# A last expert phase with eight slots cut in two halves of 64 rows, 19 slots in place of 22

## The reference

```python
logits = xf @ Wg
top_w, top_i = jax.lax.top_k(logits, TOP_K)              # TOP_K = 2, E = 8
top_w = jax.nn.softmax(top_w, axis=-1)
one_hot = jax.nn.one_hot(top_i, E, dtype=xf.dtype)
combine = jnp.einsum('nk,nke->ne', top_w, one_hot)
h = jnp.einsum('nc,ech->enh', xf, W1)                    # 256 -> 512
g = jnp.einsum('nc,ech->enh', xf, W2)
y = jnp.einsum('enh,ehc->enc', jax.nn.silu(h) * g, W3)   # 512 -> 256
out = jnp.einsum('enc,ne->nc', y, combine)
```

## Time and profile before

| | us |
|---|---|
| Runs shown (3) | 504.51, 506.26, 506.55; median 506.26 |
| Profiled execution, time | 505.15 |
| Its span | 503.4 |
| PE busy | 439.5 (87%) |
| DVE busy | 281.0 (56%) |
| ACT busy | 206.0 (41%) |
| POOL busy | 166.6 (33%) |

### The profile page before, as it was taken

One profiled execution on the slowest core, in us unless ns is written; L12 is line 12 of the kernel. 1 busy time (PEld: TensorE's weight loads), 2 busy tenths in 40 slices (PEclk: granted clock), 3 DMA queues, 4 the chain that ended last, 5 costly groups with the idle time before them and its releaser, 6 DMA issues.

```text
span 503.4 us, 9416 instructions
## 1 busy us (share of the span) xinstructions
PE 439.5 (87%) x3418; PEld 282.7 (56%) x3419; DVE 281.0 (56%) x853; ACT 206.0 (41%) x385; POOL 166.6 (33%) x140
## 2 busy tenths in 40 slices
PE   0889899798778856878899999999999999999991
PEld 0545456456455645646557666666666666566651
DVE  0498786686869999998975767346411111111110
ACT  1234653463587424246426632453333333333330
POOL 6051010010101044631434455443544442554322
PEclk9999999999967956898999999999999999999997
DMA  8999210046045100732005222341333225333211
GB/s 174 255 210 211 58 40 3 9 132 241 19 155 210 44 7 1 276 143 85 26 28 126 42 43 43 101 69 20 50 46 53 42 42 187 63 45 50 41 21 21
DMA packets 36103, 43.16 MB, mean 86 GB/s; under 512 B 5216, under 2 KB 30560, under 8 KB 35904
## 3 DMA queue, kind: packets, MB, share of 16 engines
q1 hardware_dynamic: 26384, 32.14, 22.9%
q0 software_dynamic: 7488, 10.23, 12.9%
q10 hardware_dynamic: 2192, 0.27, 0.5%
HBM read 30.96 MB, written 11.53 MB: 84 GB/s over the span
## 4 chain that ended last, share of the span: by engine, by line
PE 65%; DVE 17%; issue 5%; DMA 5%; ACT 4%; SPq 3%; POOLq 0%; DVEq 0%; ACTq 0%
PE psum L2257 26%; PE psum L2276 13%; PE psum L1874 9%; DMA M3s<-in_x_dram 4%; PE psum L2267 3%; PE psum L1888 3%; PE psum L1900 2%; PE psum L2247 2%; PE psum L1918 2%; DVE st_att L1028 1%; SPq L316 1%; DVE H L1271 1%; DVE qtok L1188 1%; DVE Eb L1068 1%; DMA out_dram<-O,dst_i 1%
## 5 line engine op out<-in xcount | busy, mean ns | idle before, releaser
L1771 DVE TENSOR_TENSOR QT<-QT,psum 128x512 f32<-128x512 f32 x39 | 26.8, 687 | 136.9 <-PE psum L2257 136.9
L2276 PE MATMUL psum<-M3s,KT 128*128 x312 | 74.1, 380 | 1.3 <-ACT KT L822 0.8
L2257 PE MATMUL psum<-M1s,KT 128*128 x156 | 74.0, 597 | 1.1 <-issue 0.8
L2257 PE MATMUL psum<-M2s,KT 128*128 x156 | 73.3, 592 | 0.0
L2276 PEld LDWEIGHTS psum<-M3s,KT 128*128 128x128 f32 x312 | 58.6, 190 | 22.1 <-issue 16.1
L833 ACT ACTIVATE O<-psum,gate_slot 128x256 f32<-128x256 f32 x39 | 18.5, 474 | 106.7 <-PE psum L2276 106.7
L1874 PE MATMUL psum<-M2s,M1s 128*128 128x512 f32 x128 | 58.7, 602 | 0.8 <-ACT H L688 0.7
L503 POOL DMA_INDIRECT KT<-mixture_rows_in,src_i x39 | 42.6, 1093 | 33.0 <-issue 19.7
L2257 PEld LDWEIGHTS psum<-M2s,KT 128*128 128x128 f32 x156 | 29.6, 190 | 37.3 <-issue 37.3
L530 POOL DMA_INDIRECT mixture_rows_out<-O,src_i x17 | 30.8, 1813 | 33.1 <-ACT O L833 13.3
L818 ACT ACTIVATE QT<-psum 128x512 f32<-128x512 f32 x39 | 23.3, 596 | 39.8 <-PE psum L2257 39.7
(11 more groups left out here) (407 smaller groups left out, 747.1 us busy)
## 6 DMA issues: line engine op xcount, KB each, us to landing
M3s<-in_x_dram SPq DMA_DIRECT2D x4, 1024.0 KB, 11.8
M3s<-in_L_ffn_W_dram SPq DMA_DIRECT2D x1, 4096.0 KB, 15.1
M2s<-in_L_ffn_W_dram SPq DMA_DIRECT2D x1, 4096.0 KB, 15.4
M1s<-in_L_ffn_W_dram SPq DMA_DIRECT2D x1, 4096.0 KB, 15.1
M3s<-in_x_dram SPq DMA_DIRECT2D x4, 992.0 KB, 15.7
M1s<-vtok SPq DMA_DIRECT2D x64, 34.0 KB, 1.9
mixture_rows_out<-H SPq DMA_DIRECT2D x4, 512.0 KB, 4.1
M1s<-in_L_tok_W_dram SPq DMA_DIRECT2D x2, 512.0 KB, 14.2
```

The costliest lines, as they stand in the source:

```text
L1771: v.tensor_tensor(sil[:, u, :], sil[:, u, :], bank[3], ALU.mult).then_inc(v_gated, 1)
L2257: last = mm(z, xrT[:, u, c, :], w[:, bass.ds(e, 1), c, :].rearrange("p a h -> p (a h)"), start=(c == 0), stop=(c == CH - 1))
L2276: last = mm(bank[6][:, 0:DM], actT[:, u, c, :], M3s[:, bass.ds(e, 1), c, :].rearrange("p a d -> p (a d)"), start=(c == 0), stop=(c == HC - 1))
```

## The change

The last phase gets 19 slots in place of 22, so there are 36 in all. Eight of them (`HALVED`: 17, 18, 20, 21, 23, 24, 26, 28) are cut: rows 0 to 63 have an expert that is looked up, rows 64 to 127 have a fixed one, expert n in the n-th such slot. Eleven are whole; four of these (19, 22, 25, 27) stand between the cut ones, seven (29 to 35) behind. `COLUMN` maps a slot's place in time to its column in the tables.

On PE each up and down product of a cut slot is issued as two matmuls, one for each half of 64 columns of the array (`experts`, and the loop over `rows`). A cut slot is delivered by two DMAs of 64 rows, `deliver` and `deliver_high`; the second waits until the first has landed, as every delivery does. `MIXED` is 29, so the copy comes after slot 28. Around it POOL takes other fetches first: no delivery stands in turn 30, and from turn 31 on delivery j-2 follows fetch j+3.

The block arithmetic is longer, the positions are moved twice (`move_left`), rows are respread (`spread_halves`) and `rows_hot` is done anew for all four groups of tiles. `places2` for the last tiles moves from behind the activations of step 12 to behind the up products of step 11; the one-hot tables move from step 13 to 14, the table matmul from step 14 to 15, the gates from 15 to 16. Slot 17's fetch, its transposes and its ACT copy come at the end of step 15, behind the down product.

```diff
-    SLOTS = (2 * NTOK + E * (P - 1)) // P
...
-    REST = SLOTS - FULL
-    WHOLE = REST - E
-    MIXED = FULL + E
+    HP = P // 2
+    WHOLE = 2 * NTOK // P - FULL - E // 2
+    REST = E + WHOLE
+    SLOTS = FULL + REST
+    ORDER = "TTWTTWTTWTWT"
+    MIXED = FULL + len(ORDER)
+    HALVED = [FULL + n for n, kind in enumerate(ORDER) if kind == "T"]
...
-            sp.wait_ge(d_deliver, 16 * MIXED)
+            sp.wait_ge(d_deliver, delivered(MIXED - 1))
...
+            def deliver_high(j):
+
+                pool.wait_ge(d_deliver, delivered(j) - 16)
+                gp.indirect_dma_start(acc, bass.IndirectOffsetOnAxis(ap=dst_high[:, COLUMN[j] - FULL:COLUMN[j] - FULL + 1], axis=0),
+                                      yrow[HP:P, j % 4, :], None, compute_op=ALU.add).then_inc(d_deliver, 16)
...
             for j in range(SLOTS):
-                if j + 3 < SLOTS:
+                split = j - 1 in HALVED
+                if split:
+                    deliver(j - 1)
+                if j + 2 == FULL:
+                    fetch(FULL)
+                if j + 3 < SLOTS and not (j + 3 == FULL):
                     fetch(j + 3)
...
-                if j > 0:
+                if split:
+                    deliver_high(j - 1)
+                elif 0 < j <= MIXED:
                     deliver(j - 1)
+                elif j > MIXED + 1:
+                    deliver(j - 2)
+            deliver(SLOTS - 2)
             deliver(SLOTS - 1)
...
-                if j + 2 < SLOTS:
+                if j + 2 < SLOTS and not (j + 2 == FULL):
                     slot_rows(j + 2, u)
...
                 slot_out(j)
+                if j + 2 == FULL:
+                    slot_rows(j + 2, u)
...
                 if j == 13:
-                    move_last(TILES)
-                    pair_slots(TILES)
-                    wrap_slots()
-                    slots_hot(2, TILES, REST, far_slot)
+                    positions(TILES, ALU.is_le, R_lim, W_at)
+                    move_left(TILES)
+                    pair_slots(TILES, halves=True)
+                if j == 14:
+                    slots_hot(2, TILES, REST, slot_in)
                     table_tiles(2, TILES, REST)
-                if j == 14:
-                    rows_of(FIRST, TS)
-                    rows_hot(3)
+                    rows_of(0, TILES)
+                    for i in range(STEPS - 1):
+                        rows_hot(i)
+                if j == 15:
+                    rows_hot(last)
                     rest_experts()
...
+            def experts(j):
+
+                n = COLUMN[j] if isinstance(j, int) else j
+                e = bass.ds(pe.value_load(exi[0:1, bass.ds(n, 1)], min_val=0, max_val=E - 1), 1)
+                if isinstance(j, int) and j in HALVED:
+                    return [(slice(0, HP), e), (slice(HP, P), slice(n - FULL, n - FULL + 1))]
+                return [(slice(0, P), e)]
...
                     for c in range(CH):
-                        last = mm(z, xrT[:, u, c, :], w[:, bass.ds(e, 1), c, :].rearrange("p a h -> p (a h)"),
-                                  start=(c == 0), stop=(c == CH - 1))
+                        for rows, e in parts:
+                            last = mm(z[rows, :], xrT[:, u, c, rows], w[:, e, c, :].rearrange("p a h -> p (a h)"),
+                                      start=(c == 0), stop=(c == CH - 1))
...
-                if j == 12:
-                    places2(2, FIRST, TILES, 1, bank[1])
...
+                if j == 11:
+                    places2(2, FIRST, TILES, 1, bank[1])
+                if j == 16:
                     gate_columns(2, TILES, REST, bank[7])
...
-                if isinstance(j, int) and j == 14:
+                if late_rows:
                     slot_tables(2, TILES, REST, bank[1])
...
                 slot_down(j, u)
+                if late_rows:
+                    slot_rows(j + 2, u, loads)
```

More of the change, by code:

```diff
@@ L298, in audio_tower_kernel, with delivered @@
         NORM2_ACT = 2
+        def delivered(j):
+            return 16 * (j + 1 + sum(h <= j for h in HALVED))
         def step_of(slot, lag):
@@ L367, in _ @@
             sp.wait_ge(d_copied, 16)
-            sp.wait_ge(d_deliver, 16 * SLOTS)
+            sp.wait_ge(d_deliver, delivered(SLOTS - 1))
         @block.gpsimd
@@ L831, in slot_out @@
                     act.wait_ge(v_gate_slot, 3)
-                wait(act, d_deliver, 16 * (j - 3))
-                a.activation(yrow[:, j % 4, :], bank[6][:, 0:DM], ACT.Copy, scale=gate_slot[:, j:j + 1]
+                wait(act, d_deliver, delivered(j - 4))
+                a.activation(yrow[:, j % 4, :], bank[6][:, 0:DM], ACT.Copy, scale=gate_slot[:, COLUMN[j]:COLUMN[j] + 1]
                              ).then_inc(a_slot_out, 1)
@@ L1466, in ranks, with whole @@
                 return ln(v.tensor_copy(ra[:, 7, lo:lo + n, :], z[:, 0:n * E].rearrange("p (t e) -> p t e", e=E)))
-            def whole(out, counts, half):
-                own(ln(v.tensor_scalar(out, counts, half, P * MAGIC, ALU.add, ALU.add)))
-                own(ln(v.tensor_scalar(out, out, P * MAGIC, 1.0 / P, ALU.subtract, ALU.mult)))
+            def whole(out, counts, half, rows=P):
+                own(ln(v.tensor_scalar(out, counts, half, rows * MAGIC, ALU.add, ALU.add)))
+                own(ln(v.tensor_scalar(out, out, rows * MAGIC, 1.0 / rows, ALU.subtract, ALU.mult)))
             def first_slots(counts, n, ts):
@@ L1582, in rest_blocks @@
[L1582 to L1585 removed]
+                whole(F, counts, -(P - 1) / 2)
+                own(ln(v.tensor_tensor(F_new, F, used, ALU.subtract)))
+                own(ln(v.tensor_tensor_scan(F_end, ones_e[:], F_new, 0.0, ALU.mult, ALU.add)))
+                own(ln(v.tensor_tensor(F_off, F_end, F_new, ALU.subtract)))
@@ new lines, in rest_blocks @@
+                ln(v.tensor_tensor(W_off, W_end, blocks, ALU.subtract))
+                own(ln(v.tensor_scalar(H_lim, W_lim, float(HP), None, ALU.add)))
+                ln(v.scalar_tensor_tensor(H_at, expert_no[:], float(P), H_lim, ALU.mult, ALU.subtract))
+                own(ln(v.tensor_tensor(over, counts, H_lim, ALU.subtract)))
+                ln(v.tensor_scalar(W_at, W_off, float(P), float(P * E - 1), ALU.mult, ALU.add))
+                own(ln(v.tensor_scalar(over, over, 0.0, None, ALU.max)))
@@ L1610, in pair_slots, with spread_halves @@
                 own()
+                if halves:
+                    spread_halves(n)
                 whole(slot_in[:, :, 0:n], rs[:, 5:7, 0:n], -(P - 1) / 2)
-            def wrap_slots():
-                ln(v.tensor_scalar(far_slot[:], slot_in, float(REST), -float(REST), ALU.is_equal, ALU.mult))
-                own()
-                ln(v.tensor_tensor(far_slot[:], far_slot[:], slot_in, ALU.add))
-                own()
+            def spread_halves(n):
+                at = rs[:, 5:7, 0:n]
+                low, half, first = (half_row[:, m, :, 0:n] for m in range(3))
+                own(ln(v.tensor_scalar(low, at, 0.0, -(HP - 1) / 2, ALU.min, ALU.add)))
+                ln(v.tensor_scalar(first, at, 0.0, float(E * P), ALU.is_lt, ALU.mult))
+                own(ln(v.tensor_scalar(half, low, HP * MAGIC, None, ALU.add)))
+                own(ln(v.scalar_tensor_tensor(half, half, -HP * MAGIC, first, ALU.add, ALU.add)))
+                own(ln(v.tensor_tensor(at, at, half, ALU.add)))
             def slots_hot(which, tiles, n, s):
@@ L2275, in slot_down @@
                 for c in range(HC):
-                    last = mm(bank[6][:, 0:DM], actT[:, u, c, :],
-                              M3s[:, bass.ds(e, 1), c, :].rearrange("p a d -> p (a d)"),
-                              start=(c == 0), stop=(c == HC - 1))
+                    for rows, e in parts:
+                        last = mm(bank[6][rows, 0:DM], actT[:, u, c, rows], M3s[:, e, c, :].rearrange("p a d -> p (a d)"),
+                                  start=(c == 0), stop=(c == HC - 1))
                 last.then_inc(p_down, 1)
```

112 lines of the change are left out of this document (60 added, 52 removed).

## The result

| | before | after |
|---|---|---|
| median of 5 runs, us | 505.14 (504.51 to 506.55) | 499.89 (499.34 to 501.6) |
| ratio, 95% interval | | 0.990 (0.9885 to 0.9914) |
| profiled execution: time / span, us | 505.15 / 503.4 | 499.34 / 497.2 |
| up products of slot 17 start at | 361.79 | 361.81 |
| up products of slot 30 start at | | 445.29 |

The change takes 5.3 us off, where 11.9 were forecast. It is faster by 1.0%, clear of the interval, and the time lies inside the range, but more than half of the gain is missing. The products came out as forecast. What failed is the size of one half delivery, the distance over the copy, and one sentence on the fetches.

A forecast was written before the change was run, and what follows sets the result against it. PE was taken as the bound, 5.82 us per step. Terms -17.5 + 3.9 + 2.3 - 0.9 + 0.3 = -11.9 us against 505.15 gave 493.3; with the median 1.1 higher, 494.4, range 490.5 to 503.5.

The forecast's parts named there:

- Three slots fewer, 17.5 us, and no cost for the halves on PE: PE's path: three steps of 5.82 us go, -17.5 us; the two column halves of cut products overlap at no cost.
- Rival 3: PE, cut slots: column halves don't overlap, 41.4 us on top, 536 us; chance 0.05.
- Switching, 13 x 0.3 = 3.9 us: PE, steps 16 to 28: each round trip between full and tiled array costs 0.3 us, +3.9 us in all.
- Deliveries, h = 3.3 us: POOL and DMA: h, the time per half delivery, is 3.3 us, with POOL's part 1.0; ends 2.6 and 4.54.
- the sign of being wrong: Half deliveries: the prediction is wrong if they land later than 3.1 us, or DMA or POOL stands between PE's steps.
- rival 1: POOL's part of a half delivery doesn't shrink: h 3.9, deliveries bound slot 17 to the end, 501.1 us; chance 0.18.
- It does, barely: Delivery chain keeps up with PE: two cut slots and a whole one need 17.7 us, PE takes 18.4.
- Debt at the end, +2.3: Past slot 28: deliveries need 41.6 us to the start of slot 35's, PE would allow 39.3; +2.3 us.
- Fetches run two steps ahead, so none is late: POOL's queue: a fetch stands between two half deliveries, yet none comes late.
- The 0.9 us behind the copy goes: Behind the copy to the output: two fetches ahead of the waiting delivery remove PE's 0.9 us delay.
- Tables, +0.3, and slot 17 at 361: Steps 11 to 16: moved table work costs +0.3 us, at worst 3; slot 17's up products start at about 361 us.
- rival 4: Steps 12 to 16: DVE or the late fetch stalls them by 1 to 3 us, 496 to 497 us; chance 0.07.

The follow-up runs named there:

- x7_swapped_fetch_first: The changed kernel with a delivery's two waits in the other order and the fetch ahead of the lower half's delivery: 494.05 us.
- x2_fetch_first: The changed kernel with only the fetch of a turn moved ahead of the lower half's delivery: 500.69 us.
- x5_waits_swapped: The changed kernel with the two waits of a delivery written in the other order: 495.68 us.
- y1_before_swapped: The kernel before the change with the two waits of a delivery in the other order: 505.87 us, ratio 1.001.
- x10_all: The changed kernel with waits swapped, fetch ahead of the lower half, two whole slots moved behind the copy, expert numbers loaded at step heads: 492.02 us.

## Why the prediction was wrong, step by step

- *Three slots fewer, 17.5 us, and no cost for the halves on PE:* right. Up products of a cut slot take 3.65 us, inside the 3.4 to 3.7 named (382.12 to 385.77). Rival 3 is out. The factor that the Trainium skill gives for three column tiles (page "TensorE: Matmul & The Clock Gate", Part 3) doesn't carry over to two of 64 columns: they overlap nearly fully, 1.94 us against 1.88.
- *Switching, 13 x 0.3 = 3.9 us:* right, measured 4.2 in time and 3.8 in the trace, together with what the halves themselves cost.
- *Deliveries, h = 3.3 us:* **the step that failed**. "Between 0.8 (half) and 1.59 (all fixed) I take 1.0" was a choice against the nearer row: the delivery's own 1.59 lay there, and the fetch's 0.99 is another kind of transfer. Measured 1.42 to 1.46. POOL's wait behind an upper half ends 3.1 to 3.2 us behind its start, where a landing at 2.55 was forecast and 3.1 named as the sign of being wrong. Against it the wait behind the landing was shorter where the transfer itself waits. Mean h 3.6, midway between forecast and rival 1 (3.9).
- *"It does, barely":* with h = 3.3 a group took 17.7 us against 18.4; a slack of 0.7 over four halves is used up at h = 3.47. The working showed that the margin was 0.2 us per half, while its own ends for h were 2.6 and 4.54. The place where a term has a threshold deserved the larger chance. Rival 1's sum, -5.2, is almost exactly what came (-5.3 in the medians), and that is in part luck. Its mechanism, a chain that binds from slot 17 to the end, holds at the end; ahead of the copy the chain was only level with PE.
- *How much of the miss h is:* from the lower half of 17 to the start of 35 the forecast had 2.3 us over PE's 106.6, rival 1 had 9.0. Measured are 112.8 (376.04 to 488.86), 6.2 over. The forecast's own sum with h = 3.6 gives 110.8, 4.2 over. So h is 1.9 of the 3.9 us that this term is short. Most of the rest are PE's late steps ahead of slot 28, 1.0, and the distance over the copy, 12.33 where h = 3.6 and 7.8 make 11.4.
- *Debt at the end, +2.3:* measured 4.3. Of the 2.0 us more, 1.2 are over the copy: the distance of 12.34 didn't shrink with the half in front of it, and half of that is the copy itself, which landed 8.9 us behind its issue and 8.3 before; 0.5 are six starts at 4.62 in place of 4.54; the half in front of the copy adds 0.1.
- *"Fetches run two steps ahead, so none is late":* wrong. Four were late, and their steps were 0.3 to 1.0 us longer than in x7_swapped_fetch_first, 2.6 us in all, since the change puts them behind a lower half that waits for ACT or for the landing before it. Taking the lateness away alone gave no time (x2_fetch_first).
- *The 0.9 us behind the copy goes:* right; steps behind it are 5.81, 5.83 and 5.82 us long.
- *Tables, +0.3, and slot 17 at 361:* 361.81, a little late. The other kernels of this study that left the slots 0 to 16 of TensorE as they are started slot 17 at 361.2 to 363.0 in their profiled runs, so this term is inside that scatter. No wait for DVE was seen where rival 4 put one.
- *The Trainium skill's page* "DMA: Bandwidth & Descriptors", section on the SWDGE path, led to h = 4.4 and no gain. Measured is 3.84 against 4.58 for the whole with the same kind of wait, and 3.43 against 4.12 in x5_waits_swapped: a half saves 0.7 us, not 0.15. The trace disagrees on how fast rows move (64 rows of 1 KB in 0.65 us), and agrees that most of a small transfer is fixed.

## What to carry to other kernels

When a change cuts one transfer in two, price its fixed part as fully fixed unless a row of the same kind shows otherwise, and write down at which price the side chain becomes the bound: a chain with a slack of 0.2 us per link is no cover. A repair on a queue is worth nothing until the queue is the bound (y1_before_swapped), and then it may be worth as much as the change. Ask also what the repair makes slower: here each swapped wait moved its pause to the other one. Ahead of a wait on a shared queue, put what others need soon.

## What the runs showed of the hardware

- **Where a wait sits matters.** By the trace's records of the packets, POOL started a delivery 1.07 us behind the last arrival of the one before when a separate instruction waited for that landing and the transfer came behind it, and 0.60 us when the transfer itself did. In distances: 3.84 to 3.43 us for halves, 4.58 to 4.12 for whole slots, with one line swapped. The wait that got the separate instruction in its place paid for it: behind ACT's end a delivery started at 0.28 us, and with the swap at 0.74 to 0.80.
- **An accumulating transfer of 64 rows costs POOL 1.42 to 1.46 us, one of 128 rows 1.55 to 1.61**; a fetch of 128 rows 1.00. The first row moves 2.0 us behind the start in both sizes.
- **Two column halves of 64 with 512 moving fp32 columns overlap nearly fully**: 1.94 us for eight against 1.88 for four on the full array.
- **A fetch issued together with a copy that fills the DMA engines landed after 9.2 us in place of 2.9** (x10_all, one fetch). That the copy is the cause is not shown.
